# 117 filler products of TensorE taken out of a four-stage graph and expert kernel

## The reference, cut to what matters

```
x = x + L0_gnn(layernorm(x))   # hyperbolic graph network, 2 layers
x = x + L0_ffn(layernorm(x))   # 8 experts, top 2 of a gate, int(1.2 * 625 / 8) = 93 rows for each
x = x + L1_gnn(layernorm(x))   # graph convolution, 2 layers, relu between
x = x + L1_ffn(layernorm(x))   # attention over pooled keys, 128 heads, then two dense layers
```

## Time and profile before

| | |
|---|---|
| median of 3 runs | 2073.5 us (2072.75 to 2074.43) |
| profiled execution, own time | 2073.17 us |
| its span | 2071.4 us |
| TensorE busy | 2054.5 us (99%), 13385 products |
| VectorE, ScalarE, GpSimd busy | 1482.0 us (72%), 1142.0 us (55%), 930.0 us (45%) |

### The profile page before, as it was taken

How to read it: one execution, slowest core, us unless ns; L and a number is a source line. 1 busy time by engine, 2 the same in 40 slices (tenths; PEclk the granted TensorE clock), 3 DMA queues, 4 the chain that set the end, 5 groups by cost and what they waited for, 6 DMA issues and landing times.

```text
span 2071.4 us, 36145 instructions
## 1 busy us (share of the span) xinstructions
PE 2054.5 (99%) x13385; PEld 1927.3 (93%) x13385; DVE 1482.0 (72%) x3084; ACT 1142.0 (55%) x3035; POOL 930.0 (45%) x707
## 2 busy tenths in 40 slices
PE   8999999999999999999999999999999999999998
PEld 7986666788899999999999999999999999999997
DVE  8779998843667667676767676666767676766776
ACT  5566778524655544555555555445555555554464
POOL 0010001201655555565656565555656565655471
PEclk9999999999999999999999999999999999999999
DMA  5305999900321111111122211111111222111110
GB/s 143 106 6 185 329 334 322 306 20 9 131 86 66 66 66 66 66 66 66 66 92 86 84 66 66 66 66 66 66 66 66 100 82 79 66 66 66 62 47 25
DMA packets 89161, 201.15 MB, mean 97 GB/s; under 512 B 8196, under 2 KB 12580, under 8 KB 88985
## 3 DMA queue, kind: packets, MB, share of 16 engines
q1 hardware_dynamic: 86746, 196.28, 27.7%
q0 software_dynamic: 2240, 2.57, 0.5%
HBM read 196.31 MB, written 2.51 MB: 96 GB/s over the span
## 4 chain that ended last, share of the span: by engine, by line
PE 96%; DVE 3%; ACT 1%; issue 0%; DMA 0%; POOL 0%; SPq 0%; DVEq 0%
PE PS L54 86%; PE PS L57 5%; PE PS L53 5%; DVE LW L60 1%; DVE JU L76 1%; DVE ACC L60 0%; DVE XFL L60 0%; DVE PO L68 0%; DMA edgi<-in_dst 0%; ACT UH L88 0%; DVE GEL L60 0%; DVE gUL L60 0%; DVE H1L L75 0%; DVE OHsx L68 0%; ACT gUH L88 0%
## 5 line engine op out<-in xcount | busy, mean ns | idle before, releaser
L54 PE MATMUL PS<-ZH,WS 128*128 128x314 f32 x4096 | 939.7, 310 | 0.0
L54 PEld LDWEIGHTS PS<-ZH,WS 128*128 128x128 f32 x4096 | 695.7, 189 | 0.0
L54 PE MATMUL PS<-ZL,WS 128*128 128x314 f32 x2048 | 626.9, 306 | 0.0
L60 DVE TENSOR_TENSOR ACC<-ACC,PS 128x314 f32<-128x314 f32 x1008 | 461.7, 475 | 197.7 <-PE PS L54 187.4
L60 POOL TENSOR_TENSOR WS<-RAW,WS 128x512 fp32r<-128x512 f32 x256 | 326.7, 1297 | 167.7 <-ACT WS L88 167.7
L54 PEld LDWEIGHTS PS<-ZL,WS 128*128 128x128 f32 x2048 | 387.0, 189 | 0.0
L60 POOL TENSOR_TENSOR ML<-MF,MH 128x400 fp32r<-128x400 f32 x124 | 129.7, 1046 | 428.2 <-ACT MH L88 428.2
L88 ACT ACTIVATE ZH<-PS,g1T 128x628 fp32r<-128x628 f32 x128 | 100.6, 786 | 255.3 <-PE PS L54 255.3
L60 POOL TENSOR_TENSOR WQ<-RAW,WQ 128x512 fp32r<-128x512 f32 x128 | 217.3, 1698 | 42.8 <-ACT WQ L88 42.8
L88 ACT ACTIVATE EE<-EE,SM 125x100 f32<-125x100 f32 x640 | 233.2, 378 | 1.2 <-DVE SM L68 1.2
L88 ACT ACTIVATE MH<-MF 128x400 fp32r<-128x400 f32 x128 | 68.2, 533 | 286.9 <-DVE MF L60 285.7
(11 more groups left out here) (366 smaller groups left out, 3648.6 us busy)
## 6 DMA issues: line engine op xcount, KB each, us to landing
RAW<-in_L_ffn_wz_w SPq DMA_DIRECT2D x66, 1024.0 KB, 5.5
RAW<-in_L_ffn_w SPq DMA_DIRECT2D x64, 1024.0 KB, 7.4
RAW<-in_L_ffn_Wq_w SPq DMA_DIRECT2D x32, 1024.0 KB, 5.5
CB<-c_rows SPq DMA_DIRECT2D x32, 195.3 KB
RAW<-in_L_gnn_W SPq DMA_DIRECT2D x4, 1024.0 KB, 16.8
RAW<-in_L_ffn_Wkv_w SPq DMA_DIRECT2D x4, 1024.0 KB, 15.1
RAW<-in_L_ffn_Wk_T SPq DMA_DIRECT2D x2, 1024.0 KB, 19.1
WB<-w_rows SPq DMA_DIRECT2D x6, 273.4 KB
```

The lines of the kernel that those rows point to most:

```text
L54: return self.q.matmul(o, l, r, start=start, stop=stop)
L60: return Nothing() if self.q is None else self.q.tensor_tensor(out=o, in0=a, in1=b, op=op)
```

## The change

All calls of `pe_busy` and the helper itself are taken out. Nothing is added or moved, and every wait stays at its place.

```diff
@@ -1001,10 +1001,6 @@
-        def pe_busy(q, bank, tile, n):
-            for _ in range(n):
-                q.mm(PS[0:94, bank, :], tile[:, 0:94], tile[:, 0:512], True, True)
-
         def pe_token_matmul(q, k, t, bank):
@@ -1095,7 +1091,6 @@
             i.then_inc(*deg_mm.up())
-            pe_busy(q, 7, UH[:, 0, :], 10)
@@ -1136,7 +1131,6 @@
                     i.then_inc(*ss_mm.up())
-            pe_busy(q, 6, W2H[:, 0, :], 21)
             q.wait_ge(*row_v.of(1, "ssu"))
@@ -1748,7 +1742,6 @@
             q.wait_ge(*w_hi.of(0, 1))
-            pe_busy(q, 3, HW[1], 17)
             turned(0)
@@ -1871,16 +1864,13 @@
             q.wait_ge(*free[7])
-            pe_busy(q, 7, HW[1], 19)
             rank_row(0)
             weights_T()
             q.wait_ge(*free[2])
-            pe_busy(q, 2, HW[1], 21)
             dispatch(0)
             rank_row(1)
             q.wait_ge(*free[1])
             gathered_T(0)
-            pe_busy(q, 1, HW[1], 4)
             for e in range(NE):
@@ -2923,24 +2913,19 @@
             q.wait_ge(*gm_v.of(1, "x", 2))
-            pe_busy(q, 2, GUH[:, 0, :], 6)
             turn(3)
-            pe_busy(q, 2, GUH[:, 0, :], 4)
             first(0)
             turn(4)
             q.wait_ge(*fx_lo.of(2))
-            pe_busy(q, 7, GUH[:, 0, :], 5)
             first(1)
             second(0)
             second(1)
-            pe_busy(q, 7, GUH[:, 0, :], 8)
             q.wait_ge(*pool_a.of("wx", 1))
...
             i.then_inc(*pool_mm.up("wxt"))
-            pe_busy(q, 5, GUH[:, 0, :], 2)
             q.wait_ge(*fx_lo.of(4))
```

## The result

The changed kernel takes 2086.25 us (median of 6, 2084.75 to 2087.63), the kernel before 2074.16 us in the same comparison (6 runs, 2072.75 to 2076.72). The difference of the medians is 12.1 us. The ratio, estimated from the runs and not the quotient of the two medians, is 1.0053, with a 95% interval of 1.0043 to 1.0063, which is 8.9 to 13.1 us: slower in either case. The forecast was 2080.9, with a range of 2075.5 to 2092.

What follows compares the result with a forecast made beforehand. TensorE was taken to bound the kernel (96% of the chain its own). Clock losses of 1.7 + 2.0 + 1.4 + 1.5 + 0.8 = 7.4 us on 2073.17 gave 2080.6, stated as the median 2080.9; range 2075.5 to 2092.

Steps and rivals of the forecast that it cites:

- forecast proper: Whole kernel: four falls of the clock, each short; 2080.9 us, band 2077.7 to 2086, chance 0.50.
- long low clock: Rival: clock stays low from 150 to about 178 us; +16.7 us, 2090.2; sign: stage over 8 us longer; chance 0.20.
- No direct gain: All 11 groups: waits take the fillers' place, so removing them gains 0, bounds 0 to -1.1 us.
- A: Rest behind the edge counts, 87.5 to 90.5, 3.0 us: no fall, cost 0 (1.7 if it falls).
- B: Rest in the second hyperbolic layer, 123.4 to 128.5, 5.1 us: falls, costs 1.7 us, bounds 0 and 3.0.
- C: Rest ahead of the gate, 146.6 to 150.8, 4.2 us: falls, costs 2.0 us, up to 6 if low throughout.
- D: Rest ahead of the rank row, 157.7 to 162.06, 4.4 us: falls or still low, +1.4 us, bounds 0 and 1.5.
- E: Rest ahead of the dispatch, 163.8 to 169.25, 5.4 us, the longest: falls, +1.5 us, bounds 0 and 3.
- G: Pooling, rest from 470.8 to 474.26 with 8 transposes inside: half a fall, 0.8 us, bounds 0 and 3.
- then rests of at most 2.2 us: Later pooling rests, the one of 2.2 us at 481.90 to 484.13; no cost of their own was listed.
- Not slower: Rival: clock never falls inside the kernel, only the direct gain of 0 to 1.1 us, 2072.4 to 2073.5; chance 0.15.
- Few falls: Rival: falls are luck, only B and E fall, 1.7 + 1.5 = 3.2 us, 2076.7; chance 0.15.

Runs made afterwards that it cites:

- e5: Kernel before with every group of fillers cut to half its count (56 in place of 117): 2076.11 us against 2074.14, ratio 1.0010.
- e11: Kernel before without only the 10 fillers behind the edge counts: 2075.49 us against 2074.09, ratio 1.0007.
- e9: Changed kernel (all 117 fillers out) plus ten early fillers, at the start and in the rest at 40.6 us: 2084.24 us, ratio 1.0049.
- e2: Kernel before without only the 61 fillers of the expert stage: 2078.01 us against 2074.43, ratio 1.0019.
- e3: Kernel before without only the 25 fillers of the pooling: 2077.35 us against 2074.43, ratio 1.0011.
- e4: Kernel before with each filler product replaced by 2.2 transposes of 128 columns, same places: 2073.07 us against 2074.43, ratio 0.9995.
- e8: Kernel before plus ten early fillers, five at the start and five in the rest at 40.6 us: 2072.77 us against 2074.14, ratio 0.9990.
- e6: Kernel before without only the pooling's last two filler groups (8 and 2): 2076.88 us against 2074.14, ratio 1.0006.
- e7: Kernel before without only the pooling's first three filler groups (6, 4 and 5): 2075.15 us, ratio 1.0001.

## Why the prediction was right

Its direction and its mechanism hold: no gain from the products taken out, and a loss by the clock alone. The size, 7.4 us forecast and 12.1 measured, was too small, mostly by one term. The measured 2086.25 us lies just above the band of the forecast proper, 2077.7 to 2086, and nearer to the long low clock's 2090.2 than to 2080.9; it lies inside the stated range because that one was 16.5 us wide. Step by step, with the stages of the profile after:

- No direct gain. Right: the first products wait for the releasers that were named, and come at the old distance from them, within 0.03 us.
- A, 0 with 1.7 if it falls; it had 1.24. Wrong side of an even choice. I put the line between fall and no fall midway between 1.7 and 4.7 us; behind the rests of 2.4 us in e5 and of 2.6 us in e11 it fell, and at 45 us even behind one of 1.3. e9 shows the rest of 2.6 us without a fall, so a length alone doesn't decide it. The two ends that I compared weren't measured alike either: 1.7 is idle time, 4.5 to 4.7 and A's 3.0 run from the start of the last product.
- B, 1.7; it had 2.15 in an execution that stayed low for 4.6 us of work. Right.
- C, 2.0, had 1.40; D, 1.4, had 1.34; E, 1.5, had 1.20. Right in sum, 4.9 against 3.9. The median of e2 says 3.6. The clock did rise between C and D, at 161.2, and did not between D and E: 168.1 to 181.6 is one stretch.
- G, 0.8, had 4.1 in the profile, above my bound of 3; e3 gives 2.9 in the median. This is the step that failed: "then rests of at most 2.2 us", taken for harmless. The second fall comes behind just such a rest, and meets the 40 products that pool the rows, which I hadn't listed as work at risk: they take 6.54 us in place of 4.71, and the ten ahead of them 2.39 in place of 1.30.
- The rivals. Not slower: out. Few falls: out, there were six, and the mean clock of all six executions is 0.989 to 0.991. Long low clock: partly so, from 168.1 to 181.6 us, but C's stage was not low throughout, and the work from C to the first expert is 3.9 us longer (28.39 us against 24.45), under the 8 us that I had named as its sign. Its reason by the Trainium skill's rule on transposes isn't borne out: in e4 they held the clock.
- The sum is against one profiled execution that had no luck against it. Executions of the kernel before differ by 3 us and more, which the prediction didn't see. The start and the rest at 42 us are where the profiles show it, and e8 takes it away. Medians share that on both sides. The 3.5 us from which I worked out B, C and E were one execution's figure; the low stretches that I met there last 3.3, 6.7 and 13.5 us.

Not settled: what decides whether a rest between 1.3 and 3 us brings a fall. It was not tried to move one rest alone by small steps.

## What to carry to other kernels

Before you take idle-looking TensorE work out, list the rests that it leaves, and behind each of them the dense work that would run at half rate; the price is half of the time that TensorE works in the low stretch, 1.2 to 2.9 us for each place here, and it can come with rests as short as 1.3 us. Ask for the granted clock by stretches of a few us, since a page of 50 us slices hides it. The start of a kernel is such a rest too: ten cheap products, five there and five in a rest at 40 us, gave 1.4 us together and took most of the spread out of the times.

## What the runs showed of the hardware that I had not expected

- 4.9 us of fp32 transposes alone held the clock at 1.00 (e4), against the Trainium skill's statement.
- Falls came behind rests of 2.0 to 2.6 us (e5, e6, e11), behind two of 1.38 and 1.00 us with four transposes between (e7), and behind one of 1.3 us followed by small products (at 45 us in the kernel after, e6, e7 and e11), while 1.7 us at 26 us brought none in any profile. The same rest of 2.6 us at 90 us was followed by a fall in the kernel after and not in e9.
- A low stretch can begin when TensorE is already at work again: 157.8 in the kernel after, 0.7 us behind the first transposes; 488.7 in e6, 0.2 us behind the first of the 40 pooling products.
- The same kernel rises from the low level at its start at different moments, 8.5 us in the profile of before and near 11 in that of after, and at 28 us that execution is 1.0 us behind.
